# Xattn pair kernel: phi G of two batches as one product of 512 columns, and v from row sums carried through DRAM

## The reference

```
q = x w_q^T;  k = ctx w_k^T;  v0 = ctx w_v^T
x1 = x + alpha * softmax(q k^T / sqrt(512)) v0 w_o^T
# second stage, channels first: 256 channels, 512 positions, 128 inner channels
g = (g_w ctx + g_b)^T;  theta = (theta_w x1 + theta_b)^T;  phi = phi_w ctx + phi_b
y = (theta phi / 512) g
out = batchnorm(w_w y^T + w_b) + x1
```

## Time and profile before

| | us |
|---|---|
| median of 3 runs | 388.99 (388.89 to 389.0) |
| profiled execution, whole | 389.22 |
| its span from first to last instruction | 387.3 |
| PE busy in the span | 382.2 |
| DVE busy | 306.8 |
| ACT busy | 199.1 |

### The profile page before, as it was taken

The page is one execution under the profiler, slowest core; times in us unless marked ns, Lnnn a source line. Parts: engine busy times, 40 slices in busy tenths (PEclk is TensorE's granted clock), DMA queues, the critical chain, the costliest instruction groups (busy, mean ns, idle before and its releaser), DMA issues.

```text
span 387.3 us, 5597 instructions
## 1 busy us (share of the span) xinstructions
PE 382.2 (99%) x1827; PEld 321.5 (83%) x1827; DVE 306.8 (79%) x596; ACT 199.1 (51%) x411; POOL 1.3 (0%) x6
## 2 busy tenths in 40 slices
PE   8999999999999999999999999999999999999995
PEld 5888888888888888888888888888888888888885
DVE  4899788986698677986798867985798867986786
ACT  3477567432764257542665247451675338451553
POOL 1000000000000000000000000000000000000000
PEclk9999999999999999999999999999999999999999
DMA  8975742485474646546383555655375464024523
GB/s 244 376 294 211 268 122 54 157 297 189 131 247 119 234 136 216 187 139 217 107 269 111 190 169 167 231 158 187 120 241 161 162 190 135 27 82 154 145 83 108
DMA packets 56507, 68.13 MB, mean 176 GB/s; under 512 B 4656, under 2 KB 47408, under 8 KB 53424
## 3 DMA queue, kind: packets, MB, share of 16 engines
q1 hardware_dynamic: 55776, 67.07, 52.6%
q10 hardware_dynamic: 720, 0.92, 0.7%
HBM read 49.09 MB, written 18.87 MB: 175 GB/s over the span
## 4 chain that ended last, share of the span: by engine, by line
PE 96%; DMA 1%; DVE 1%; ACT 0%; ACTq 0%; issue 0%
PE bank L354 23%; PE bank L355 23%; PE bank L356 23%; PE bank L408 8%; PE bank L427 7%; PE bank L394 5%; PE bank L416 4%; PE bank L449 2%; DMA cT_raw<-w_q 1%; PE bank L453 1%; DVE xb L1095 0%; DVE xb L1090 0%; ACTq L614 0%; ACT t_sides L611 0%; ACT theta_hi L611 0%
## 5 line engine op out<-in xcount | busy, mean ns | idle before, releaser
L355 PE MATMUL bank<-c_sides,qk_hi 128*128 128x512 f32 x128 | 49.9, 390 | 0.0
L356 PE MATMUL bank<-c_sides,qk_lo 128*128 128x512 f32 x128 | 49.9, 390 | 0.0
L354 PE MATMUL bank<-ov_hi,c_sides 128*128 128x512 f32 x128 | 49.9, 390 | 0.0
L355 PE MATMUL bank<-ov_lo,c_sides 128*128 128x512 f32 x128 | 49.9, 390 | 0.0
L354 PE MATMUL bank<-c_sides,qk_hi 128*128 128x512 f32 x128 | 49.8, 389 | 0.0
L356 PE MATMUL bank<-ov_hi,c_sides 128*128 128x512 f32 x128 | 49.8, 389 | 0.0
L611 ACT ACTIVATE t_sides<-bank 128x512 fp32r<-128x512 f32 x32 | 19.0, 594 | 37.6 <-PE bank L356 37.6
L408 PE MATMUL bank<-t_sides,xT_hi 128*128 128x512 f32 x128 | 31.9, 391 | 0.0
L611 ACT ACTIVATE probs<-bank 128x512 f32<-128x512 f32 x16 | 9.4, 586 | 38.6 <-PE bank L416 38.6
L845 DVE TENSOR_TENSOR t_sides<-bank,t_sides 128x512 fp32r<-128x512 f32 x32 | 22.0, 687 | 8.9 <-ACT t_sides L611 8.9
L704 ACT ACTIVATE probs<-probs,neg_max 128x256 f32<-128x256 f32 x32 | 16.1, 502 | 24.1 <-DVE neg_max L961 24.1
(11 more groups left out here) (147 smaller groups left out, 835.9 us busy)
## 6 DMA issues: line engine op xcount, KB each, us to landing
cT_raw<-ctx_t SPq DMA_DIRECT2D x8, 1024.0 KB, 5.9
xT_raw<-x_t SPq DMA_DIRECT2D x8, 1024.0 KB, 4.8
c_raw<-ctx_n SPq DMA_DIRECT2D x8, 1024.0 KB, 6.8
xb<-x SPq DMA_DIRECT2D x16, 512.0 KB, 4.1
out<-xb SPq DMA_DIRECT2D x14, 512.0 KB, 2.8
gram_moved<-gram_blocks SPq DMA_DIRECT2D x16, 256.0 KB, 2.3
gram_blocks<-gram_moved SPq DMA_DIRECT2D x64, 64.0 KB, 2.0
moved<-blocks SPq DMA_DIRECT2D x16, 256.0 KB, 2.3
```

What stands on the lines that cost most here:

```text
L354: pe.matmul(dst, ahi, bhi, start=(k == 0), stop=False)
L355: pe.matmul(dst, ahi, blo, start=False, stop=False)
L356: mm = pe.matmul(dst, alo, bhi, start=False, stop=(k == k_tiles - 1))
```

## The change

- `gram` is laid out as [tile of contraction, batch, 256 columns], without the column of sums and the padding, so one product reads both batches as 512 contiguous columns. `phi_gram` does 6 products of 512 columns, into one bank of PSUM in place of two, and waits for both batches' G.
- `phi_squares` transposes 512 columns in one instruction, and the v instructions are gone.
- The row sums go to a tile of their own, `c_sum`. SP stores it to DRAM (`send_sums`) and loads the 512 sums of the pair back to every partition as rows (`fetch_sums`), into a part of `row` that is free after the start. phi's weights are loaded once as rows too (`phi_rows`).
- DVE multiplies the rows of sums by phi's rows (`weigh_sums`), and ACT sums each product with the bias spread over its 256 elements (`v_sums`), which gives v.
- Waits on `v_made` on PE become waits on `phi_turned`.

```diff
 ROW_PHI_B, ROW_GAMMA, ROW_VAR, ROW_ALPHA, N_ROW = 0, CI, CI + L, CI + 2 * L, CI + 2 * L + 1
-GW = S + 2
...
 wg_bias = sb("wg_bias", [P, L])
+gram_raw = sb("gram_raw", [P, 2, KS, S])
+gram = split("gram", [P, KS, 2, S])
+phi_rows = sb("phi_rows", [P, S])
...
 v = sb("v", [P, 2])
-gram_raw = sb("gram_raw", [P, 2, KS, GW])
-gram = split("gram", [P, 2, KS, GW])
+c_sum = sb("c_sum", [P, 2 * KS])
+sums_moved = nc.dram_tensor("sums_moved", [2, P, KS], F32).ap()
+sum_rows = row[:, ROW_GAMMA:ROW_GAMMA + 2 * S].rearrange("p (b s) -> p b s", b=2)
...
 VO_BANK = [[2, 3], [6, 7]]
-PHI_BANK, FIRST_PHI_BANK = [2, 3], [6, 7]
+PHI_BANK, FIRST_PHI_BANK = 2, 6
...
+    def send_sums():
+        sp.dma_start(sums_moved.rearrange("b p k -> p b k"), c_sum[:].rearrange("p (b k) -> p b k", b=2)).then_inc(sums_stored, 16)
+    def fetch_sums():
+        sp.dma_start(row[:, ROW_GAMMA:ROW_GAMMA + 2 * S],
+                     sums_moved.rearrange("b p k -> (b p k)").partition_broadcast(P)).then_inc(sums_loaded, 16)
...
     sp.dma_start(g_raw, g_w).then_inc(small_w_loaded, 16)
+    sp.dma_start(phi_rows[:], phi_n).then_inc(phi_rows_loaded, 16)
...
         send(gram_moved[b], gram_blocks[:, b], gram_stored[b])
+    sp.wait_ge(c_summed, 4)
+    send_sums()
...
         fetch(gram_blocks[:, b], gram_moved[b], gram_loaded[b])
+    sp.wait_ge(sums_stored, 16)
+    sp.wait_ge(bn_step, 8)
+    fetch_sums()
...
     load_xT(1)
-    sp.wait_ge(c_summed, 4)
...
         two, four = counts(sp, p, 2, [1, 2, 3, 4]), counts(sp, p, 4, [1, 2, 3, 4, 8])
-        turned = counts(sp, p, 16, [16, 32])
+        turned, turns = counts(sp, p, 16, [16, 32]), counts(sp, p, 1, [2])
+        def next_sums():
+            sp.wait_ge(sums_stored, turned[32])
+            sp.wait_ge(v_made, two[2])
+            fetch_sums()
...
             send_squares(0)
-            sp.wait_ge(phi_blocks_made, two[2])
+            sp.wait_ge(phi_turned, 1)
...
             next_x(1)
+        if not first and not last:
+            sp.wait_ge(c_summed, four[8])
+            send_sums()
...
             if not first:
-                sp.wait_ge(c_summed, four[8])
...
                 fetch(gram_blocks[:, b], gram_moved[b], gram_loaded[b])
+        if first:
+            sp.wait_ge(c_summed, four[8])
+            send_sums()
+            load_c(p + 2)
+        if not last:
+            next_sums()
         if prefetch:
-            if first:
-                sp.wait_ge(c_summed, four[8])
-                load_c(p + 2)
...
             store(p, 0)
-            sp.wait_ge(phi_blocks_made, two[4])
+            sp.wait_ge(phi_turned, turns[2])
...
-    def phi_gram(b, banks=PHI_BANK):
-        product(bank[banks[b]][:, 0:GW], lambda k: cut(phi_w, every, k, every),
-                lambda k: cut(gram, every, b, k, every), KS).then_inc(phi_done, 1)
+    def phi_gram(to_bank):
+        product(bank[to_bank][:].rearrange("p (b s) -> p b s", b=2), lambda k: cut(phi_w, every, k, every),
+                lambda k: cut(gram, every, k), KS).then_inc(phi_done, 1)
...
             pe.wait_ge(small_lo, 2)
-            for b in range(2):
-                pe.wait_ge(gram_lo, b + 1)
-                phi_gram(b, FIRST_PHI_BANK)
+            pe.wait_ge(gram_lo, 2)
+            phi_gram(FIRST_PHI_BANK)
...
         else:
-            pe.wait_ge(v_made, two[2])
+            pe.wait_ge(phi_turned, p + 1)
...
         if first:
-            pe.wait_ge(v_made, two[2])
+            pe.wait_ge(phi_turned, p + 1)
...
         pe.wait_ge(tT_lo, four[5])
-        for b in range(2):
-            pe.wait_ge(gram_lo, two[b + 3])
-            phi_gram(b)
+        pe.wait_ge(gram_lo, two[4])
+        phi_gram(PHI_BANK)
...
                 act.activation(c_raw[:, b, k], c_raw[:, b, k], ACT.Identity,
-                               accum_out=gram_raw[:, b, k, S:S + 1]).then_inc(c_summed, 1)
+                               accum_out=c_sum[:, b * KS + k:b * KS + k + 1]).then_inc(c_summed, 1)
...
         act.wait_ge(gram_done, count)
-        hi(gram_raw[:, b, i, 0:S], bank[GRAM_BANK[b][i]][:, S:2 * S], cross_copied)
+        hi(gram_raw[:, b, i], bank[GRAM_BANK[b][i]][:, S:2 * S], cross_copied)
...
         hi(ov[0][:, m, :], bank[KH + m][:], ov_hi, scale=row[:, ROW_ALPHA:ROW_ALPHA + 1])
-    act.wait_ge(pad_zeroed, 1)
...
             act.wait_ge(phi_done, pairs_read)
-        hi(gram[0][:, b], gram_raw[:, b], gram_hi)
+        hi(gram[0][:, :, b], gram_raw[:, b], gram_hi)
...
     act.activation(neg_max[:, 0], std_col[:], ACT.Exp)
-    act.wait_ge(c_summed, 4)
...
         loads = counts(act, p, 16, [32])
-        landed = counts(act, p, 16 * BLOCKS, [16 * BLOCKS])
+        landed, pairs_done = counts(act, p, 16 * BLOCKS, [16 * BLOCKS]), counts(act, p, 1, [1])
...
                phi_blocks[:].rearrange("p q x a -> p x q a"), u_hi)
+        def v_sums():
+            act.wait_ge(sums_weighted, two[2])
+            for b in range(2):
+                act.activation(sum_rows[:, b], sum_rows[:, b], ACT.Identity, bias=phi_bias[:],
+                               accum_out=v[:, b:b + 1]).then_inc(v_made, 1)
...
+        if not first:
+            v_sums()
...
         low_scores(1)
-        if not first:
+        if first:
+            v_sums()
+        else:
...
         theta_part(1)
-        act.wait_ge(c_summed, four[8])
         for b in range(2):
-            gram_part(b, four[4 + KS * (b + 1)], two[b + 1])
+            gram_part(b, four[4 + KS * (b + 1)], pairs_done[1])
...
                 gram_blocks[:, b, :, i * KS:(i + 1) * KS].rearrange("p j k a -> p k j a"),
-                gram_raw[:, b, i, 0:S].rearrange("p (k j i) -> p k j i", k=KS, i=SQUARE))
+                gram_raw[:, b, i].rearrange("p (k j i) -> p k j i", k=KS, i=SQUARE))
...
     dve.tensor_scalar(g_bias[:], g_bias[:], col[:, G_B:G_B + 1], None, ALU.mult).then_inc(g_bias_made, 1)
-    dve.tensor_scalar(phi_bias[:], col[:, PHI_B:PHI_B + 1], float(H), None, ALU.mult).then_inc(bn_step, 1)
+    dve.tensor_scalar(phi_bias[:], col[:, PHI_B:PHI_B + 1], float(H) / S, None, ALU.mult).then_inc(bn_step, 1)
...
         for k in range(KS):
-            whole = gram_raw[:, b, k, 0:S].rearrange("p (i q a) -> p i q a", i=KS, q=BLOCKS)
+            whole = gram_raw[:, b, k].rearrange("p (i q a) -> p i q a", i=KS, q=BLOCKS)
...
     def gram_part(b, count):
-        lo(gram, gram_hi, count, (every, b), gram_raw[:, b], gram_lo)
-    for b in range(2):
-        gram_close(b, 16 * BLOCKS, b + 1)
-        gram_part(b, b + 1)
+        lo(gram, gram_hi, count, (every, every, b), gram_raw[:, b], gram_lo)
+    def weigh_sums(landed):
+        dve.wait_ge(sums_loaded, landed)
+        for b in range(2):
+            dve.tensor_tensor(sum_rows[:, b], sum_rows[:, b], phi_rows[:], ALU.mult).then_inc(sums_weighted, 1)
+    gram_close(0, 16 * BLOCKS, 1)
+    gram_part(0, 1)
+    gram_close(1, 16 * BLOCKS, 2)
+    dve.wait_ge(phi_rows_loaded, 16)
+    weigh_sums(16)
+    gram_part(1, 2)
...
         landed = counts(dve, p, 16 * BLOCKS, [16 * BLOCKS, 32 * BLOCKS])
+        pairs_done = counts(dve, p, 1, [2])
...
-        def phi_squares(b, count, banks=PHI_BANK):
+        def phi_squares(count, from_bank):
             dve.wait_ge(phi_done, count)
-            dve.transpose(phi_blocks[:, :, b * KS:(b + 1) * KS].rearrange("p j x a -> p x j a"),
-                          bank[banks[b]][:, 0:S].rearrange("p (k j i) -> p k j i", k=KS, i=SQUARE)
-                          ).then_inc(phi_blocks_made, 1)
-            dve.tensor_scalar(v[:, b:b + 1], bank[banks[b]][:, S:S + 1], phi_bias[:], None,
-                              ALU.add).then_inc(v_made, 1)
+            dve.transpose(phi_blocks[:].rearrange("p j x a -> p x j a"),
+                          bank[from_bank][:].rearrange("p (x j i) -> p x j i", x=2 * KS, i=SQUARE)
+                          ).then_inc(phi_turned, 1)
...
                     at = phi_blocks[:, :, b * KS + k]
-                    dve.scalar_tensor_tensor(out=at, in0=phi_b, scalar=gram_raw[:, b, k, S:S + 1], in1=at,
+                    dve.scalar_tensor_tensor(out=at, in0=phi_b, scalar=c_sum[:, b * KS + k:b * KS + k + 1], in1=at,
...
+        if not first:
+            weigh_sums(loads[16])
...
         if first:
-            phi_squares(0, 1, FIRST_PHI_BANK)
-            phi_squares(1, 2, FIRST_PHI_BANK)
+            phi_squares(1, FIRST_PHI_BANK)
...
         tT_part(3, four[8])
-        phi_squares(0, two[3])
-        phi_squares(1, two[4])
+        phi_squares(pairs_done[2], PHI_BANK)
...
     pool.memset(g_bias[:], 1.0).then_inc(ones_made, 1)
-    pool.memset(gram_raw[:], 0.0).then_inc(pad_zeroed, 1)
...
 "g_w": a[l1 + "g_w"],
+"phi_n": a[l1 + "phi_w"].reshape(CI, KS, P).transpose(0, 2, 1).reshape(CI, S),
...
```

More of the change, by code:

```diff
@@ L29, with two_stage_cross_attention @@
 ROW_PHI_B, ROW_GAMMA, ROW_VAR, ROW_ALPHA, N_ROW = 0, CI, CI + L, CI + 2 * L, CI + 2 * L + 1
-GW = S + 2
-def two_stage_cross_attention(nc, x, x_t, ctx_n, ctx_t, w_q, w_k, w_v, w_o_t, g_w, phi_w_t, theta_w_t,
```

(8 more changed lines are left out.)

## The result

| | before | after |
|---|---|---|
| median, us | 389.0 (388.7 to 389.26) | 395.86 (395.56 to 397.38) |
| profiled execution, us | 389.22 | 397.38 |
| its span, us | 387.3 | 395.6 |
| granted clock, mean | 1.00 | 0.991 |

The ratio is 1.0183 [1.0166, 1.0199]: 6.9 us slower, where 0.83 us faster was forecast. The forecast missed in sign, and the time lies far outside the range.

What follows compares the result with a forecast made beforehand. PE, busy 99% of the span and without gaps in the loops, was taken as the bound. Only the products' gain counted, the rest being hidden: 388.99 - 0.83 = 388.16 us, range 387.9 to 388.9.

Steps and rivals of the forecast that it cites:

- Part 1: phi G products, 12 of 258 columns becoming 6 of 512: 0.10 us gained per block, 0.83 us for 8 blocks.
- (a): Only the phi G block shortens, or new products take 0.232 us: 0.6 us off, 388.4 us; chance 0.21.
- (b): A product's fixed cost is small, as the skill page has it: 0.2 us off, 388.8 us; chance 0.04.
- Parts 2 and 3: DVE's transpose and multiplications, ACT's two sums per pair fit idle time; ACT margin 0.4 to 1.0 us, priced at nothing.
- Rival (d): ACT's margin at the head of pairs 1 to 7 is used up, 0.3 us lost each: 390.3 us; chance 0.03.
- Part 4: SP's new store of sums and broadcast load per pair: about 0.4 us of SP each, no new wait in the loop.
- xT of pair 2 ... is wanted a pair later: In pair 0 SP waits some 2 us for the sums' store; the xT load behind it is needed only later.
- Part 5: At the start the broadcast goes out at 41.5 to 42.0 and lands in 2.3 to 3 us: no stall.
- threshold of 3.8 us: At the start, the broadcast does no harm if it lands within 3.8 us after its issue.
- rival (c): The start's broadcast lands too late, first pair stalls: at 6.4 us, PE 2.6 us late, 390.8 us; chance 0.10.

Runs made afterwards that it cites:

- run 7: The kernel of run 6 plus the 2 KB stores of sums in 8-byte runs, which nobody waits for until the end: 392.74 us, ratio 1.0081.
- run 6: Changed kernel with the 512-column products alone: sums not stored, fetched or multiplied, v zero: 389.13 us, ratio 0.9994.
- kernel 8: Changed kernel with the sums stored as 128 runs of 16 bytes in place of 256 of 8: 392.52 us, ratio 1.0092.
- run 9: The kernel of run 4 plus 16-byte runs, and pair 0's broadcast sent between the stores and fetches of G: 388.66 us, ratio 0.9981.
- Run 3: Changed kernel with pair 0 in the loop's order, sums stored ahead of the cT load: 395.48 us, ratio 1.0167.
- run 4: Changed kernel with sums used late and sent late at the start, and pair 0 in the loop's order: 390.79 us, ratio 1.004.
- Run 5: Changed kernel with 13 products of constants ahead of PE's wait at the first phi G: 396.8 us, ratio 1.0185.
- 11: The kernel of run 9 with 12 waits, six more SP instructions, ahead of pair 0: 388.67 us, ratio 0.9987.
- 12: The kernel of run 9 with 24 waits, 12 more PE instructions, ahead of the first products: 390.91 us, ratio 1.0021.

## Why the prediction was wrong

**Part 1, the products: right.** 1.36, 1.36 and 4.99 us as forecast, 0.107 us for a block. Rivals (a) and (b) are out, and with them the 0.2 us by the sizes in the Trainium skill, page "TensorE: Matmul & The Clock Gate", section "Back-to-back issue gap".

**Parts 2 and 3, DVE and ACT: right.** The transpose of 512 columns from PSUM takes 0.72 us (taken: 0.71), the two multiplications 0.75. ACT's two sums run from 231.28 to 232.38, and the copy of the low scores starts at 233.12, with 0.75 us of idle time that PE ends. The margin is 0.7 us, inside the 0.4 to 1.0. Rival (d) did not come.

**Part 4 is where it failed:** "Each occupies SP for about 0.4 us like its neighbours" was the whole price of the store. It counted the issue and not the landing, and nothing for the neighbours. The issue was 0.38 us in most pairs, but 0.90 at the start; the landing was 4.2 to 7.4 us; and the stores by themselves cost the kernel 3.6 us (run 7 against run 6). I had taken the landing by bytes: 2 KB must be quicker than 256 KB. Runs 8 and 9 show that the form of the store decides: with the same 2 KB in 128 runs of 16 bytes it lands after 1.4 us in place of 3.6 where nothing is ahead of it. The page "DMA: Bandwidth & Descriptors" of the Trainium skill, section "Specifications", which I had cited, says that a piece under 512 bytes is done as a read and a write. The late landings go the way of that rule, but no run shows the mechanism, and it doesn't give the size: 16-byte runs are under 512 bytes too. The rule spoke against the change and I gave it no rival and no chance: that was the choice at fault. No row of before had a store of such short runs, so the upper end of this term was unknown and not 0.4 us.

**Also Part 4: "xT of pair 2 ... is wanted a pair later"** followed the load to its reader and not to its neighbours. SP's wait was 3.2 us (2 forecast), but its cost was in the queue: a load of 1 MB, issued 9 us later than before (4.5 of them because the whole pair was late), stood ahead of the phi store of 256 KB, which landed after 6.8 us. Run 3 takes the wait away and leaves 4.4. The rest has two more causes, each enough to make this store late by itself: the small store just ahead of the loads (run 7, without any broadcast: 5.1 us) and the broadcast just ahead of them (run 4: 5.0 us), which Part 4 priced by its issue too. With none of the three it is 2.3 (run 6) and 2.5 (run 9). Together they are 2.7 + 1.6 us of the loss in the profiled execution, and no rival had them.

**Part 5, the start, was sized wrong in three terms.** Issue of the broadcast 43.39 (41.5 to 42.0 forecast), landing 5.6 us (2.3 to 3), so the stall was 3.16 us. The threshold of 3.8 us and the rival (c) named the right mechanism; it got 0.10. Its price of 2.6 us left out the clock: in the profiled execution the products behind each of the two long gaps run at the lower level and cost 1.6 to 1.8 us more. Run 5 shows that this follows PE's pause: without the pause it was not there. In the time of the kernel it counts for less, as the three executions without a dip show.

**The sum** then was 389.22 - 0.86 + 4.93 (start) + 4.30 (pair 1) = 397.6 for a profiled execution of 397.38.

**Open.** Which part of a transfer's way the small store holds; whether it is the number or the length of its runs; why the fetch in pair 1 is held just when the 16 KB of instructions are loaded. In size the gap behind the hold would take back the gain in run 6 (0.80 us against 0.86) and part of it in run 9, but no run removed the hold, so that is not shown. Before, a fetch at 98.43 took 0.66 us in the same place and cost nothing.

## What to carry to other kernels

Don't price a store by its bytes: look at the form of its runs. Here 2 KB in runs of 8 bytes landed later than 256 KB in runs of 512, and held whatever was issued beside it. So lay a small store out in fewer and longer runs, and send it where nothing is due. Where a load is moved, look at which urgent transfer it will stand ahead of, not only at when its own data is wanted. A broadcast of 256 KB ahead of urgent transfers is not free either. And a long gap on a bound PE can bring time at the lower clock behind it: here up to 1.8 us for each gap, of which the whole kernel lost less.

## What the runs showed of the hardware

- 256 runs of 8 bytes (2 KB) to DRAM land after 4.2 to 7.4 us (kernel after), 128 of 16 bytes after 2.7 to 5.3 us (kernel 8). With nothing ahead of them it is 3.6 us (kernels 3 and 4) and 1.4 us (9, 11 and 12).
- A load of 1 MB issued right behind such a store lands after 8.2 us (8-byte runs, kernel 4) or 6.1 us (16-byte runs, kernel 9), and after 4.9 us without one (kernel 6). The second store of G (256 KB) lands after 2.4 us, and after 4.4 to 5.3 us with the 8-byte store issued 0.4 us behind it.
- A broadcast of a 2 KB row to 128 partitions (256 KB written) lands after 3.0 to 6.1 us.
- In the profiled executions PE's gaps of 2.4 to 3.5 us were each followed by the lower clock; those of up to 1.7 us in the pairs were followed by 0.1 us of excess or less.
- One issue of a DMA in each kernel took SP 1.2 to 2.1 us (0.66 in the kernel before) in place of 0.43, beside one of the six loads of 16 KB of instructions; beside the other five none took over 1.3 us.
